# Attention: second chunk projected in the lead, and the causal mask of the row maxima added by VectorE

## What is computed

```python
B, T, C, H, hd = 8, 256, 128, 16, 8
qkv = layernorm(x) @ w_qkv.T + b_qkv
att = einsum('bhqd,bhkd->bhqk', q, k) / sqrt(hd) + bias     # bias: per head, from the positions
att = where(causal, att, -inf)
out = einsum('bhqk,bhkd->bhqd', softmax(att), v)
x = x + out @ w_proj.T + b_proj
```

## Time and profile before

| | us |
|---|---|
| time, median of 3 runs (lowest to highest) | 1125.52 (1120.83 to 1126.85) |
| time of the profiled execution | 1125.59 |
| its span | 1123.9 |
| PE busy in the span | 972.7 |
| DVE busy | 934.7 |
| ACT busy | 778.1 |
| POOL busy | 762.9 |

### The profile page before, as it was taken

One profiled execution on the slowest core, in us unless ns is written; L12 is line 12 of the kernel. 1 busy time (PEld: TensorE's weight loads), 2 busy tenths in 40 slices (PEclk: granted clock), 3 DMA queues, 4 the chain that ended last, 5 costly groups with the idle time before them and its releaser, 6 DMA issues. The chain is left out here.

```text
span 1123.9 us, 25541 instructions
## 1 busy us (share of the span) xinstructions
PE 972.7 (87%) x9861; PEld 511.5 (46%) x9861; DVE 934.7 (83%) x1729; ACT 778.1 (69%) x1707; POOL 762.9 (68%) x425
## 2 busy tenths in 40 slices
PE   4789999999999999999999999793677999997585
PEld 1334444444444444444444444342354566664354
DVE  5688999999999999999899999986994466664995
ACT  5888898888988988889889888852331355544341
POOL 3497988889899888899898888982451223321342
PEclk9899999999999999999999999987888599997687
DMA  6553454436444445445344443403720001000001
GB/s 229 208 170 134 147 140 140 145 111 192 153 134 152 135 142 161 136 150 153 134 153 134 151 134 127 159 20 84 154 41 0 4 18 21 20 2 2 1 1 38
DMA packets 65624, 121.66 MB, mean 108 GB/s; under 512 B 40032, under 2 KB 47008, under 8 KB 56224
## 3 DMA queue, kind: packets, MB, share of 16 engines
q1 hardware_dynamic: 65504, 120.03, 34.5%
HBM read 112.15 MB, written 6.29 MB: 105 GB/s over the span
## 5 line engine op out<-in xcount | busy, mean ns | idle before, releaser
L935 POOL TENSOR_TENSOR prod<-hid,c_rep 128x1024 f32<-128x1024 f32 x256 | 600.8, 2369 | 74.9 <-DVE hid L866 74.2
L866 DVE TENSOR_TENSOR_SCAN hid<-decay,acc 128x256 f32<-128x256 f32 x1024 | 606.6, 662 | 46.6 <-PE acc L530 46.2
L745 ACT ACTIVATE decay<-delta,a_neg 128x255 f32<-128x255 f32 x1024 | 431.6, 501 | 77.9 <-DVE hid L866 77.6
L530 PE MATMUL acc<-b_diag,du_t 64*64 64x256 f32 x4096 | 274.4, 387 | 29.1 <-DVE hid L866 26.8
L553 PE MATMUL ring<-prod,ident 64*64 64x512 f32 x2048 | 246.0, 596 | 4.0 <-POOL prod L935 4.0
L530 PEld LDWEIGHTS acc<-b_diag,du_t 64*64 64x64 f32 x4096 | 145.1, 134 | 183.6 <-issue 76.0
L1759 POOL TENSOR_SCALAR_AFFINE_SELECT att_probs<-att_probs 128x512 f32<-128x512 f32 x64 | 40.6, 634 | 126.5 <-ACT att_probs L1803 126.5
L553 PEld LDWEIGHTS ring<-prod,ident 64*64 64x64 f32 x2048 | 79.3, 135 | 101.8 <-issue 82.6
L1803 ACT ACTIVATE att_probs<-acc 128x384 f32<-128x384 f32 x128 | 55.8, 488 | 76.8 <-PE acc L1557 76.8
L437 PE MATMUL ring<-xpad,diag_cw 64*64 64x512 f32 x512 | 60.5, 589 | 0.4 <-ACT xpad L644 0.4
L1555 PE MATMUL acc<-att_qk 17*128 17x256 f32 x256 | 56.0, 456 | 0.5 <-ACT att_probs L1803 0.4
(11 more groups left out here) (175 smaller groups left out, 1333.9 us busy)
## 6 DMA issues: line engine op xcount, KB each, us to landing
c_rep<-c_rows SPq DMA_DIRECT2D x64, 1024.0 KB, 4.9
b_diag<-diag_rows SPq DMA_DIRECT2D x64, 512.0 KB, 3.8
diag_rows<-prod SPq DMA_DIRECT2D x2, 2048.0 KB, 13.7
att_qk<-in_pos_q SPq DMA_DIRECT2D x4, 768.0 KB
att_qk<-in_pos_k SPq DMA_DIRECT2D x4, 768.0 KB
att_qk<-att_dense SPq DMA_DIRECT2D x24, 64.0 KB
resid<-in_x SPq DMA_DIRECT2D x4, 256.0 KB, 3.1
c_rows<-bc SPq DMA_DIRECT2D x64, 8.0 KB, 1.5
```

What stands on the lines that cost most here:

```text
L530: last = nc.tensor.matmul(inj[m * HALF:(m + 1) * HALF, K % 2, at:at + HALF * SG], du_t[rows, n % 2, e, chans:chans + HALF], b_diag[rows, K ...
L745: last = nc.scalar.activation(decay[:, K % DECAYS, s, 1:], delta[:, n % 2, h, e * SEQ + 1:(e + 1) * SEQ], ACT.Exp, scale=a_neg[:, lay(n) % ...
L866: last = nc.vector.tensor_tensor_scan(hid[:, K % HIDS, s, :], decay[:, K % DECAYS, s, :], rows[:, s, :], 0.0, ALU.mult, ALU.add)
L935: nc.gpsimd.tensor_tensor(prod[:, K // 4 % 2, h, :, at], hid[:, K % HIDS, :, :], c_rep[:, g, :, at], ALU.mult).then_inc(s_prod, 1)
```

## The change

There are two parts. The first moves work: with `EARLY = 2`, chunk 1 is normalised and projected in the lead (iterations -3 to 0: x, q, k, v), and chunk `c + 2` within chunk `c`. The second replaces the mask products: DVE computes the maxima from `scores + mask`, with one `tensor_tensor_reduce` for each head and query tile, which also writes the masked scores into a scratch tile `masked`. Each of these is two instructions on DVE, the pass itself and one that writes the result of the reduction. `masks` is 256 columns wide, 128 of zeros and then the mask.

```diff
+EARLY = 2
...
         if 0 <= u and u % per == 9:
-            piece("v", u // per + 1, CHUNKS)
+            piece("v", u // per + EARLY, CHUNKS)
...
         for kind, when in (("x", 2), ("q", 6), ("k", 8)):
             if 0 <= u and u % per == when:
-                piece(kind, u // per + 1, CHUNKS)
+                piece(kind, u // per + EARLY, CHUNKS)
+    if -S_LEAD <= u <= 0:
+        at.append(("xqkv"[u + S_LEAD], 1))
...
-                def mask_scores(u):
-                    banks.wait_free(t, "s", u)
-                    for i in range(2):
-                        nc.tensor.matmul(diagonal(score_bank(u)[:, i:i + 1, 0:SPAN])[:, 0], ident_b[:, :], mask_b[:, :, :],
-                                         start=True, stop=False, skip_group_check=True)
...
-                        mask_scores(s)
+                        banks.wait_free(t, "s", s)
...
-                    nc.vector.tensor_reduce(npk[:, g % 2, 0, at], score_bank(u)[:, :, 0:P], AX, ALU.max, negate=True)
-                    last = nc.vector.tensor_reduce(npk[:, g % 2, 1, at], score_bank(u)[:, :, P:SPAN], AX, ALU.max, negate=True)
+                    for i in range(2):
+                        for c, (cols, hidden) in enumerate(((slice(0, P), masks[:, P:]), (slice(P, SPAN), masks[:, :]))):
+                            scores, col = score_bank(u)[:, i, cols], js[i] * STRIP + MAX_ROW
+                            last = nc.vector.tensor_tensor_reduce(masked[:, (2 * u + i) % 4, cols], scores, hidden, -1.0, -NEG, ALU.add, ALU.min,
+                                                                  npk[:, g % 2, c, col:col + 1])
...
                 moments(0)
                 normalise(0)
+                moments(1)
                 tiles.wait(v)
-                for g in range(HGROUPS):
+                add_strips(0)
+                v.wait_ge(s_maskb, 2)
+                normalise(1)
+                for g in range(1, HGROUPS):
                     add_strips(g)
                 values(0)
```

More of the change, by code:

```diff
@@ L1450, in sb @@
             return core.sb(f"att_{name}", shape, dt, stage)
-        ident_b = sb("ident_b", [P, P], BF16)
-        mask_b = sb("mask_b", [P, 2, P], BF16)
+        masks = sb("masks", [P, 2 * P])
+        masked = sb("masked", [P, 4, SPAN])
         xT = sb("xT", [P, CH])
@@ L1545, in score @@
                     if tile == 0:
-                        return nc.tensor.matmul(out[:, 0:P], q[:, 0:P], k[:, 0:P], start=False, stop=True, skip_group_check=True)
-                    return nc.tensor.matmul(out[:, P:SPAN], q[:, P:], k, start=False, stop=True, skip_group_check=True)
+                        return nc.tensor.matmul(out[:, 0:P], q[:, 0:P], k[:, 0:P], start=True, stop=True)
+                    return nc.tensor.matmul(out[:, P:SPAN], q[:, P:], k, start=True, stop=True)
                 def score_turned(u, i, tile):
@@ L1630, in _ @@
                 project_v(0)
-                t.wait_ge(s_maskb, 2)
                 for u in ITERATIONS:
@@ L1690, in peaks @@
                     b, hg, js = where(u)
-                    g, at = u // 2, slice(js[0] * STRIP + MAX_ROW, js[1] * STRIP + MAX_ROW + 1, STRIP)
+                    g, js = u // 2, where(u)[2]
                     banks.wait_filled(v, "s", u)
@@ L1734, in _ @@
                             add_row(n)
-                    if 0 <= u and u % per == 2 and u // per + 1 < CHUNKS:
-                        normalise(u // per + 1)
+                    if 0 <= u and u % per == 2 and u // per + EARLY < CHUNKS:
+                        normalise(u // per + EARLY)
                     for kind, n in work:
@@ L1746, in _ @@
                             values(n)
-                    if 0 <= u and u % per == 0 and u // per + 1 < CHUNKS:
-                        moments(u // per + 1)
+                    if 0 <= u and u % per == 0 and u // per + EARLY < CHUNKS:
+                        moments(u // per + EARLY)
             @block.gpsimd
@@ L1768, in _ @@
                 tiles.wait(p)
-                nc.gpsimd.tensor_copy(ident_b[:, :], ident[:, :]).then_inc(s_maskb, 1)
-                nc.gpsimd.tensor_copy(mask_b[:, :, :], tiles.mask[:, :].unsqueeze(1).broadcast_to([P, 2, P])).then_inc(s_maskb, 1)
-                out_bias(0)
+                nc.gpsimd.memset(masks[:, 0:P], 0.0).then_inc(s_maskb, 1)
+                nc.gpsimd.tensor_copy(masks[:, P:], tiles.mask[:, :]).then_inc(s_maskb, 1)
+                for c in range(EARLY):
+                    out_bias(c)
                 for u in range(UNITS):
                     causal(u)
-                    if u % per == 3 and u // per + 1 < CHUNKS:
-                        out_bias(u // per + 1)
+                    if u % per == 3 and u // per + EARLY < CHUNKS:
+                        out_bias(u // per + EARLY)
             @block.scalar
@@ L1819, in _ @@
                 rstd(0)
+                rstd(1)
                 copy_x(0)
@@ L1824, in _ @@
                         exps(u)
-                    if 0 <= u and u % per == 1 and u // per + 1 < CHUNKS:
-                        rstd(u // per + 1)
+                    if 0 <= u and u % per == 1 and u // per + EARLY < CHUNKS:
+                        rstd(u // per + EARLY)
                     for kind, n in iteration(u):
```

## The result

| | before | with the change |
|---|---|---|
| median, us | 1125.16 | 1145.22 |
| lowest to highest, runs | 1120.83 to 1126.85, 4 | 1137.72 to 1149.6, 4 |
| profiled execution: time, span | 1125.59, 1123.9 | 1141.87, 1140.2 |
| TensorE's granted clock, mean of the span | 0.937 | 0.914 |

In these four runs the change makes the kernel **slower, by a factor of 1.0174 (95% interval 1.0148 to 1.0201)**; the interval is clear of 1 and has 1.02 within it. I had forecast 1114.3 us and 28 in 100 for slower. The time lies inside the range of 1107 to 1149, near the end that rivals A and C had set.

A forecast was written before the change was run, and what follows sets the result against it. PE was taken to bound the attention, busy 153 of 155 us. Savings of 4.65, 2.3, 1.9 and 2.5 us over the chunks, together 11.3, took 1125.6 to 1114.3 us; range 1107 to 1149.

The forecast's parts named there:

- rival A: Attention pairs: DVE's longer passes become the bound, from P = 1.65 us on; +22, 1148 us; 15 in 100.
- rival C: Last two chunks: without whole-array mask products PE's clock falls to 1.2 GHz, 6.26 us a pair; 1149 us; 13 in 100.
- 126 us with grant 1.00 through every kind of pair: Argument that PE's clock would hold: the earlier trace showed full clock for 126 us.
- Removing the masks of a plain pair: 3.95 us: Plain attention pair at full clock: 4.26 us less 0.31, as only one of two mask steps is on the path.
- P = 1.40 us: DVE's time for the maxima of one unit: 1.10 us of passes and 0.30 of column writes, up from 0.94.
- rival B: DVE's column writes wait until the pass ahead has emptied; P = 1.72, no change, 1126.5 us; 14 in 100.
- The third chunk no longer carries projections, -2.3: Third chunk's attention loop: its pairs no longer hold a chunk's projections on PE, saving 2.3 us.
- first chunk -2.5: First chunk's seven pairs, some at the lower clock, lose mask steps; with normalisation and lead +0.3, saving 2.5 us.
- 4.65: Last two chunks: 15 plain pairs each 0.31 us shorter without masks, saving 4.65 us.
- -1.9: Second chunk: masks removed save 3.1 us, moments and normalisation behind DVE's passes give back 1.2; net -1.9 us.
- rival D: First chunk: the lead's projections keep the clock at 2.4 GHz, 6.4 us more saved; 1108 us; 8 in 100.
- The sum: All chunks' terms together: -11.3 us from the profiled 1125.6, giving 1114.3 us.

The follow-up runs named there:

- change_again: The changed kernel without an edit, run ten times: five runs at 1115.22 to 1119.5 us, five at 1139.33 to 1151.3 us.
- narrow_products: `shadow_products` with each added product on 17 rows of the array in place of 128: 1116.19 us, 0.993 of the kernel before.
- path_products: The changed kernel with overwritten mask products only in the units whose turned scores do not wait for ACT: 1133.6 us, 1.0073 of the kernel before.
- shadow_products: The changed kernel with overwritten mask products only in every other unit, whose turned scores wait for ACT: 1112.45 us, 0.9899 of the kernel before.
- scores_first: The changed kernel, no added product, both heads' scores issued ahead of the turned ones in odd iterations: 1114.64, 1140.63, 1147.16 and 1149.19 us.
- products_kept: The changed kernel with both mask products of each unit put back on PE, overwritten by the scores: 1120.67 us, 0.9947 of the kernel before.
- first_filled: `scores_first` plus overwritten products where PE waits for DVE in the first units and before the third chunk: one run 1106.47 us, five 1126.4 to 1143.55.
- early_only: The kernel before with only the projections moved, mask products and plain maxima kept: 1118.8 us, 0.9948 of the kernel before.

## Why the prediction was wrong, by its own steps

- **"Argument against rival C: 126 us with grant 1.00 through every kind of pair." This step failed.** Each pair in those 126 us still held its masks, so they told nothing of a pair without. Every term of the sum from the first chunk on took the clock of the trace before for granted, and C got 13 in 100. The clock is part of what the change changes. What the runs showed in its place: without the products PE was granted 0.50 for 85.2 us, and a pair took 6.28 us there in place of 3.93. Rival C's price was right, 6.28 us for a forecast 6.26. That its total of 1149 came near the 1145.22 was luck in part, since its place was wrong: it had fifteen pairs of the last two chunks low, the profile has eleven of the first and second, and in `change_again` the low stretches behind the first lay elsewhere. Its reason, products over the whole array, fell with `narrow_products`.
- **"Removing the masks of a plain pair: 3.95 us."** Right: 3.93 and 3.94. Of two mask steps one is worth 0.33 and the other nothing, by `path_products` and `shadow_products`.
- **"P = 1.40 us."** Too high: 1.12. The four writes, taken at 0.075 each, overlap the next pass. With it fall **rival A**, which needed P past 1.65, and **rival B**, which let the writes wait for an empty engine. That a pass of 0.42 us is followed after 0.34 stands against what the Trainium skill, "VectorE: DVE Perf Modes", section "The DRAIN you can't avoid", says first, that the next operation waits for the empty pipe, and agrees with its addition that one which is not held starts earlier. In these rows it holds even for the write of what the pass ahead has reduced.
- **"The third chunk no longer carries projections, -2.3; first chunk -2.5."** The last two chunks, at full clock, took 65.5 us from addition to addition (975.19 to 1040.71) where it had been 72.6 (949.50 to 1022.12): -7.1, for 4.65 + 2.3 = 6.95, so those terms are right. The first chunk's can only be tested where the clock came back soon, in the fast run of `scores_first`, which has the same products: low from 879 to 903 us, then at 1.00. There the second chunk's eight pairs took 35.3 us for 37.5 before, -2.2 for a forecast -1.9, but the first seven pairs 40.5 for 40.0, where my terms give -2.8 without the lead. The way to the first addition grew by 0.8 us, not 0.3. What I left out is what the move does to the clock: beside held products it is worth some 8 us, and the low stretches of the first chunk differ, 879 to 896 us with it and 873 to 897 without; that makes only a part of the 8 us. That was rival D, a part of the truth beside the forecast and not against it.
- **The sum.** Where the change's clock was granted 0.940 to 0.943 in the mean, it took 1115.2 to 1119.5 us, and the forecast was 1114.3. Their median is 5.5 us below the kernel before on that chip, half of the 11.3 forecast. The first chunk's terms, too good by some 3 us, are a part of that; the rest is open, since no trace of such a run of the change was kept. The large miss is the clock, which multiplies all of them and was not asked about.

What stays open: how much PE must do for the grant to stay at 1.00 was not measured, only that one product in a pair's shadow tips it. Why half of the runs of one program hold, and what chooses the later stretches where others fall, is open too, and so is whether the chip has a part: its ten runs are of one chip, and the record does not name that of the result. So is why one projection brings the clock back and another doesn't; that the move takes them out of the last two chunks, where a low stretch then lasts longer, is read from the traces and was not tried by itself. For the first fall, at about 880 us, the pauses speak louder than the missing products: `products_kept` fell there with all its products, and `first_filled` did not fall there with none. That is one trace of each, and `early_only` had the pauses without the fall.

The Trainium skill, "TensorE: Matmul & The Clock Gate", section "Part 1: The HAM clock gate", tells of the same two levels, and of pauses of PE as what lowers the clock. The trace agrees on the levels, 0.50 and 1.00; for the 85.2 us at 0.50 with PE busy in 85.09 of them, a pause is no explanation, nor for the fall at 977.5 us in `change_again`, ahead of which PE is busy in 37.50 of 37.50 us.

## What to carry to other kernels

Before taking small products from TensorE, ask what they do for its granted clock: a stretch of full clock in the trace speaks only for the work that it holds. A product that stood in ACT's shadow cost nothing here (3.93 us a pair with and without), and two of them in a pair were worth 17 us against the change's median over ten runs (1129.42) and 33 against its four of the result (medians, and those ten runs are of another chip); keep them, or put cheap ones there, even where their result is thrown away. Judge such a change by several runs with the grant of each, since one program can give two times nearly 3% apart.

## What the runs showed of the hardware that was not expected

- TensorE stayed at 1.2 GHz for 85 us with instructions in flight 99.9% of the time (85.09 of 85.20), and returned behind a projection over the whole array, where five others had not brought it back; with such stretches the whole kernel takes 2.7% longer, by the two halves of `change_again` (medians 1118.66 and 1148.91).
- Products of 17 rows of the array kept the clock at 1.00 from 907 us to the last addition, as those of 128 rows did from 896 (1116.19 and 1112.45 us).
- The pass of the maxima with the added mask takes 0.28 to 0.29 us for 128 columns and 0.42 for 256, and the next one starts 0.21 or 0.34 us after its start. Reading the accumulator takes 0.08 us and starts with the next pass; 256 columns are followed after 0.34 us, as a plain reduction of 256 elements is the earlier trace rows, so the second instruction cost nothing here.
